# Part of one basis combination moved into earlier pauses, the segment-maximum's key work moved ahead of the weight preparations, and the last biases added as rounded matmul rows

## The chip, the cores and the metric

One Trainium2 chip, one of its cores. Five engines run their own instruction streams and meet at semaphores: PE (matmul and transposes), DVE (VectorE), ACT (ScalarE), POOL (GpSimd) and SP, which here only issues DMAs. The metric is the device time of one execution in microseconds (us), as the median of several runs. Positions in the trace are us from the first instruction.

## The reference

Four graph layers in a row on 625 nodes with 512 features and 10,000 edges sorted by destination; each adds its result to `x`. What the change touches are the first and the last:

```python
# L0: attention over edges, softmax per destination node, then a feed-forward part
logits = einsum('ehd,ehd->eh', q[src], k[dst]); a = logits + dist_attn + path_attn
mx = segment_max(a, dst)                       # the "maximum"
e = exp(a - mx[dst]); s = segment_sum(e, dst); msg = v[src] * (e / s[dst])
...
# L3: two relational layers; w[r] is a sum over 30 bases of 512 x 512
w = einsum('rb,bio->rio', att, basis)          # r = 2 relations
...
return agg + x @ root + bias
```

The second layer of L3 uses `basis2`, `att2` and `bias2`. Nothing in `w` depends on the nodes, so the kernel forms it whenever an engine is free. L2's weights are also prepared ahead (products and transposes of `W_self`, `W_fwd`, `W_bwd`).

## The kernel before

Nodes are five tiles of 128 (`NC`), edges 84 tiles of 128 (`NT`), feature columns four blocks of 128 (`K4`). All order is written by hand: each engine's stream is a straight list, and semaphores name what it waits for.

The stretch of the change is the first third. In order of the program:

- **Sorting and projections.** DVE ranks edges in batches (`inner_ranks`, `places`); PE computes q and k in two blocks `project(0)` and `project(1)` of 64 matmuls each, between which DVE takes the next ranks. POOL sends each batch's 16 columns of edge rows to DRAM with indirect DMAs (L727, 80 in all), then loads the sorted table `att` (L733).
- **Pairs.** All node pairs' products go to DRAM by SP (`pair_d`, ten DMAs of 1.25 MB, L593).
- **v.** Five tiles; DVE adds the bias (L1314) and SP stores `v_d` (L599). PE has two PSUM slots for them, so tile m+2 waits until DVE took tile m. SP first issues the first three of the L2 weight loads (`early_in`, L597).
- **Gathers.** POOL gathers 84 tiles of logits from `pair_d` (L740), then v rows (L749), 21 tiles ahead of their use.
- **Run of bases.** `combine_run` (L1328) multiplies the 30 lower halves of `basis2` by two factors each into `acc_run`: two instructions of 1,024 columns for each base (L1335 for the first, L1341 for the others). SP loads them into three buffers, 0.5 MB each (`load_run`, L583). SP issues base 0 to 2 after `v_d`; bases 3 to 29 stand behind a wait for the landing of `v_d` and of the pairs, and behind the load of `Wo` (L606).
- **Preparations.** At the same time PE works on the 15 parts in `EARLY`: eight are 16 transposes (L1822), six are 16 f32 products (L1820), and the last product is cut in three (L1804). ACT takes each result out of PSUM (`take_early`, L869) and issues the weight load for the part three later (L871). A product needs the transposed part before it.
- **Maximum.** Logits and segment keys are turned to 112 rows by twelve transposes (L1921); ACT copies both out (L909, L911). DVE makes penalties where the key changes (L1363 to L1365), runs two scans (L1369, L1370), collects the ends of each row, and PE turns these (L1928). DVE then joins the rows on one lane (L1383 to L1404), PE turns the carries back (L1933), and DVE scans again, takes the maximum and subtracts it.
- **Messages.** PE adds 84 weighted tiles (L1976) of v rows.

In the last two layers (l = 3, 4 of `LAYERS`) `own` starts the sums of layer 3 with an f32 matmul of one row of ones and the bias (L2185); `bias2` is instead added to `xs` by one POOL instruction (L804) in layer 4's preparation.

## Time and profile before

| | us |
|---|---|
| median of 3 runs | 1359.07 |
| lowest, highest | 1354.73, 1360.41 |
| the profiled execution | 1360.03 |
| its span, first to last instruction | 1358.3 |
| TensorE clock granted over it (share of full) | 0.93 |

| engine | busy, us | share |
|---|---|---|
| PE | 1174.0 | 86% |
| DVE | 862.2 | 63% |
| ACT | 436.0 | 32% |
| POOL | 424.6 | 31% |

The shares average over stages with different limits, so the argument reads single stretches: who was idle, and which row ended that. A timeline row is start, duration, engine, line, operation, and in brackets the idle time before it with what ended it. A chain row is start, duration and what the end of the program hung on at that time.

### The profile page before, as it was taken

What the parts mean: (1) busy time and instruction counts of PE and PEld (TensorE: products, weight loads), DVE (VectorE), ACT (ScalarE), POOL (GpSimd) and SP (SyncE); (2) the same over time, 40 slices, a digit from 0 to 9 for tenths busy, and PEclk for the clock granted to TensorE, in tenths of its full rate; (3) what the DMA queues carried; (4) which work ended last, traced back from release to release, by engine and by line L of the source; (5) the groups of instructions that cost most, each with busy time, mean ns of one, the idle gap of its engine ahead of it and who ended that gap; (6) DMA issues with size and microseconds to landing.
All of it is one profiled execution on the core that took longest, in us unless ns stands there. A gap on an engine that the chain in (4) does not pass through costs nothing.

```text
span 1358.3 us, 15202 instructions
## 1 busy us (share of the span) xinstructions
PE 1174.0 (86%) x5421; PEld 822.1 (61%) x5440; DVE 862.2 (63%) x1405; ACT 436.0 (32%) x618; POOL 424.6 (31%) x405
## 2 busy tenths in 40 slices
PE   5597768847997799999897998899799998989996
PEld 4364344423543477544457997568587886778884
DVE  7618425767775649786569996636869697482211
ACT  2315121212111722100328995543232324233320
POOL 3878677772774001110037771000000000010000
PEclk8799888977999899999978999999799999899898
DMA  6215799994764024531124112034545554222001
GB/s 213 54 12 193 232 383 344 332 341 172 244 180 123 31 78 128 193 99 63 49 48 147 43 44 97 1 112 165 184 147 208 176 195 172 102 84 102 0 0 38
DMA packets 74337, 187.82 MB, mean 138 GB/s; under 512 B 14423, under 2 KB 17468, under 8 KB 69029
## 3 DMA queue, kind: packets, MB, share of 16 engines
q1 hardware_dynamic: 45044, 100.34, 21.3%
q0 software_dynamic: 21600, 64.66, 15.8%
q10 hardware_dynamic: 7632, 22.02, 4.4%
q8 instruction: 38, 0.62, 0.2%
q14 instruction: 23, 0.18, 0.0%
HBM read 149.93 MB, written 36.97 MB: 138 GB/s over the span
## 4 chain that ended last, share of the span: by engine, by line
PE 57%; DVE 17%; DMA 11%; ACT 5%; issue 5%; POOL 2%; SPq 2%; ACTq 0%; DVEq 0%; PEldq 0%
PE ps L2160 25%; DMA work<-in_L_gnn_basis 7%; PE ps L2065 5%; PE ps L2123 4%; PE ps L2055 4%; PE ps L1976 3%; DVE aux L1676 3%; PE ps L1878 3%; DVE work L1341 2%; POOL aux L749 2%; PE ps L2035 2%; DMA pair_d<-aux 2%; PE ps L1851 2%; DMA xs<-in_x 2%; PE ps L2108 2%
## 5 line engine op out<-in xcount | busy, mean ns | idle before, releaser
L2160 PE MATMUL ps<-work_r,hT_r 128*128 128x512 f32 x600 | 195.9, 408 | 2.1 <-DVE att_r L1648 1.4
L2160 PEld LDWEIGHTS ps<-work_r,hT_r 128*128 128x128 f32 x600 | 114.9, 194 | 32.9 <-issue 4.7
L2160 PE MATMUL ps<-work_r,att_r 128*128 128x512 f32 x300 | 121.2, 404 | 0.0
L727 POOL DMA_INDIRECT etab_d<-aux,edge x80 | 99.2, 1241 | 49.2 <-issue 49.2
L1652 DVE TENSOR_TENSOR bT_r<-bT,fT_r 128x512 fp32r<-128x512 f32 x50 | 38.7, 774 | 106.7 <-ACT fT_r L1065 106.7
L1676 DVE SCALAR_TENSOR_TENSOR aux<-aux,attb 128x1024 f32<-128x1024 f32 x84 | 103.1, 1278 | 2.4 <-DMA aux<-in_L_gnn_basis 2.4
L1341 DVE SCALAR_TENSOR_TENSOR work<-work,attb 128x1024 f32<-128x1024 f32 x58 | 72.0, 1296 | 42.1 <-DMA work<-in_L_gnn_basis 42.1
L2160 PE MATMUL ps<-fT_r,wA_r 128*128 128x512 f32 x250 | 87.0, 416 | 10.8 <-DVE bT_r L1652 10.8
L740 POOL DMA_INDIRECT lg<-pair_d,reli x84 | 86.2, 1026 | 29.1 <-issue 25.3
L1976 PE MATMUL ps<-work,hT_r 128*128 128x512 f32 x168 | 85.5, 642 | 8.8 <-DVE work L1424 6.5
L1820 PE MATMUL ps<-wA 128*128 128x512 f32 x160 | 77.3, 646 | 16.0 <-DMA wA<-in_L_gnn_W_bwd 6.2
L1494 DVE TENSOR_SCALAR work<-iota,srcf,flag 128x640 bf16<-128x640 f16 x168 | 64.3, 447 | 37.8 <-PE ps L2036 37.6
L2160 PE MATMUL ps<-fT_r,aux_r 128*128 128x512 f32 x250 | 80.7, 400 | 3.6 <-DVE bT_r L1652 3.6
L2123 PE MATMUL ps<-work_r 128*128 128x256 f32 x280 | 70.3, 288 | 10.3 <-DVE wA_r L1582 10.3
L749 POOL DMA_INDIRECT aux<-v_d,srcx x64 | 70.4, 1100 | 19.5 <-issue 18.6
L2065 PE MATMUL ps<-wA,aux 128*128 128x512 f32 x160 | 73.1, 599 | 1.3 <-issue 1.3
L2123 PE MATMUL ps<-wA_r,work_r 128*128 128x256 f32 x280 | 69.3, 288 | 0.0
L782 POOL DMA_DIRECT2D work<-early_d x9 | 5.4, 602 | 200.3 <-PE ps L2160 134.4
L1820 PEld LDWEIGHTS ps<-wA 128*128 128x128 f32 x160 | 32.6, 207 | 57.7 <-issue 46.3
L2160 PEld LDWEIGHTS ps<-work_r,att_r 128*128 128x128 f32 x300 | 58.1, 194 | 14.4
L2160 PEld LDWEIGHTS ps<-fT_r,wA_r 128*128 128x128 f32 x250 | 49.4, 197 | 26.1 <-DVE bT_r L1652 12.7
L778 POOL DMA_INDIRECT fT<-u_d,dstx x36 | 40.6, 1127 | 77.4 <-DMA u_d<-bT 66.7
(396 smaller groups left out, 2646.0 us busy)
## 6 DMA issues: line engine op xcount, KB each, us to landing
aux<-in_L_gnn_basis SPq DMA_DIRECT2D x44, 512.0 KB, 3.9
work<-in_L_gnn_basis SPq DMA_DIRECT2D x30, 512.0 KB, 9.5
fT<-in_L_gnn_basis POOLq DMA_DIRECT2D x24, 512.0 KB, 4.4
wA<-in_L_gnn_basis SPq DMA_DIRECT2D x22, 512.0 KB, 3.9
work<-early_d POOLq DMA_DIRECT2D x9, 1024.0 KB, 5.9
wA<-in_L_gnn_W_self ACTq DMA_DIRECT2D x7, 1024.0 KB, 14.9
pair_d<-aux SPq DMA_DIRECT2D x5, 1280.0 KB, 14.0
early_d<-work ACTq DMA_DIRECT2D x5, 1024.0 KB, 16.9
```

The costliest lines, as they stand in the source:

```text
L727: pool.indirect_dma_start(out=etab_d, out_offset=bass.IndirectOffsetOnAxis(ap=row[:, t:t + 1], axis=0), in_=etab[:, t, :], in_offset=None) ...
L740: pool.indirect_dma_start(out=lg[:, t, :], out_offset=None, in_=pair_d, in_offset=bass.IndirectOffsetOnAxis(ap=reli[:, t:t + 1], axis=0)). ...
L749: pool.indirect_dma_start(out=ring[t % RING], out_offset=None, in_=v_d, in_offset=bass.IndirectOffsetOnAxis(ap=srcx[:, t:t + 1], axis=0)). ...
L1341: ins = dve.scalar_tensor_tensor(acc_run[:, r], bas_run[b % 3], factor, acc_run[:, r], ALU.mult, ALU.add)
L1494: last = dve.tensor_scalar(hotS[:, 4 * k + j, :], iota16[:, :], srcf[:, at], flag[:, r, at], ALU.is_equal, ALU.mult)
L1676: ins = dve.scalar_tensor_tensor(acc[:, r], bas[u], factor, acc[:, r], ALU.mult, ALU.add)
L1820: last = pe.matmul(to[:, k], w[:, o, k * P:(k + 1) * P], early_s[:, o, :], start=o == 0, stop=o == K4 - 1)
L1976: pe.matmul(ps[:, bass.ds(c * 512, D)], one, msg[:, j, :], start=False, stop=False, skip_group_check=True)\
L2055: last = pe.matmul(o, w, h[:, k, nodes], start=k == i == 0, stop=(k, i) == (K4 - 1, 2))
L2065: last = pe.matmul(plan.slot(ps, "ffn2", m), node(g1T, j, m), w2s[:, j, :], start=j == 0, stop=j == 15)
L2123: last = pe.matmul(ps[:, 512 * m:512 * m + NF], hotL[k][:, j, m * P:(m + 1) * P], part[:, 4 * k + j, :], start=False, stop=False)
L2160: last = pe.matmul(o, lhsT, rhs, start=start and n == 0, stop=stop and n == 2)
```

## The change

It has five parts.

1. **Bases.** The first 12 bases (`AHEAD_RUN`) load into buffers that are free from the start, behind the last parameter loads on SP. DVE combines 0 to 5 after `places(1)` and 6 to 11 after `places(2)`. The loads of 12 to 16 stand behind the pair stores, ahead of the first weight loads; DVE combines 12 to 15 between the tiles of v, base 16 after the keys are laid out, base 17 inside the key work, 18 to 29 behind it.
2. **Keys first.** Keys are turned, copied, made into penalties and seams before the preparations; the logits come after all of them. `s_ends`, `s_soft`, `s_akT` and `s_endT` count one or two events more.
3. **Last part whole.** `ASKING` is 15: the last product is prepared as the others, not cut in three.
4. **Bias rows.** `rows_r` holds each bias of L3 as a rounded row and its rest, multiplied by two rows of ones in rounded f32, in layer 3 and in layer 4.
5. **Buffers** of the ends, chains and carries move.

```diff
+AHEAD_RUN = 12
@@ SP
+            load_run(range(AHEAD_RUN))
             for n in range(2 * NC):
...
+            sp.wait_ge(s_place, 5)
+            load_run(range(AHEAD_RUN, AHEAD_RUN + 5))
             sp.wait_ge(s_pre_job, pre.number("v", NC - 1))
             for n in range(3):
                 sp.dma_start(early_in[n], early_source(n)).then_inc(s_early_in[n], 16)
             sp.wait_ge(s_pre_dve, NC)
             sp.dma_start(v_d.rearrange("(m p) n -> p m n", p=P), vf).then_inc(s_v_out, 16)
-            sp.wait_ge(s_place, 5)
-            load_run(range(3))
             sp.wait_ge(s_v_out, 16)
...
-            load_run(range(3, NBASE))
+            load_run(range(AHEAD_RUN + 5, NBASE))
@@ POOL, layer 4
-                if l == LAYERS - 1:
-                    pool.wait_ge(s_norm, seen(5))
-                    pool.wait_ge(s_l3par, 6 * 16)
-                    pool.tensor_tensor(xs[:, :, :], xs[:, :, :], rows[:, 1, :].unsqueeze(1).to_broadcast([P, NC, D]), ALU.add).then_inc(s_added, 1)
@@ ACT
+            act.wait_ge(s_akT, 1)
+            act.activation(kT, ps[0:112, 2048:2048 + 768], ACT.Copy).then_inc(s_ak, 1)
             for part in range(ASKING):
                 take_early(part)
@@ DVE
             places(1)
+            dve.wait_ge(s_attb, 32)
+            combine_run(range(6))
             inner_ranks(range(8, 12))
             places(2)
+            combine_run(range(6, AHEAD_RUN))
...
                 dve.tensor_tensor(vf[:, m, :], pre.slot(ps, "v", m)[:, 0:D], bv, ALU.add).then_inc(s_pre_dve, 1)
+                if m < NC - 1:
+                    combine_run([AHEAD_RUN + m])
...
             dve.tensor_copy(kp.rearrange("p g t h -> p t g h"),
                             segk[:, :].rearrange("p (t g) -> p t g", g=TG).unsqueeze(3).to_broadcast([P, TT, TG, H])).then_inc(s_soft, 1)
+            first = AHEAD_RUN + NC - 1
+            combine_run(range(first, first + 1))
+            dve.wait_ge(s_ak, 1)
             step(dve.memset(pen[:, :], 0.0))
...
+            combine_run(range(first + 1, first + 2))
             dve.wait_ge(s_endT, 1)
+            dve.tensor_copy(*turned_ends(2, 3)).then_inc(s_ends, 1)
...
+            combine_run(range(first + 2, NBASE))
@@ DVE, layer 0
+                    step(dve.tensor_copy(ones_r, ones[0:2, :]))
+                    for j in range(2):
+                        step(dve.tensor_copy(bias_upper, rows[0:2, j, :]))
+                        step(dve.tensor_tensor(rows_r[0:2, j, :], rows[0:2, j, :], bias_upper, ALU.subtract))
+                        step(dve.tensor_copy(rows_r[0:1, j, :], bias_upper[0:1]))
@@ PE
-            prepare(range(ASKING))
+            pe.wait_ge(s_soft, 1)
+            for g in range(TG):
+                last = pe.transpose(ps[0:112, 2048 + g * P:2048 + (g + 1) * P], kp[:, g].rearrange("p t h -> p (t h)"), ident[:, :])
+            last.then_inc(s_akT, 1)
+            prepare(range(1))
+            pe.wait_ge(s_ends, 1)
+            turn_ends((2, 3, 4))
+            pe.wait_ge(s_ak, 1)
+            pe.wait_ge(s_ends, 2)
+            prepare(range(1, ASKING))
@@ PE, own
-                if l == 3:
-                    pe.wait_ge(s_l3par, 6 * 16)
-                    pe.matmul(o, ones[0:1, :], rows[0:1, 0, :], start=True, stop=False)
+                if l >= 3:
+                    pe.matmul(o, ones_r, rows_r[0:2, l - 3, :], start=True, stop=False)
```

Three places show the new order. On SP's queue, before, from the last pair store:

```order
L593 DMA pair_d<-aux 128x2560 [waits s_pair_dve,s_pair_act]
L597 DMA wA<-in_L_gnn_W_self 128x4x512 [waits s_pre_job]
L597 DMA wA<-in_L_gnn_W_self 128x4x512
L597 DMA wA<-in_L_gnn_W_fwd 128x4x512
L599 DMA v_d<-aux 128x5x512 [waits s_pre_dve]
L583 DMA work<-in_L_gnn_basis 128x2x512 [waits s_place]
L583 DMA work<-in_L_gnn_basis 128x2x512 x2
L606 DMA aux<-in_L_gnn_Wo 128x4x512 [waits s_pair_out2,s_pair_out3,s_pair_out1,s_wo,s_pair_out0,s_v_out]
L583 DMA work<-in_L_gnn_basis 128x2x512 [waits s_bas_used0]
```

The same place of the changed kernel; the last row loads base 17:

```order
L597 DMA pair_d<-aux 128x2560 [waits s_pair_dve,s_pair_act]
L586 DMA work<-in_L_gnn_basis 128x2x512 [waits s_place]
L586 DMA work<-in_L_gnn_basis 128x2x512 x2
L586 DMA work<-in_L_gnn_basis 128x2x512 [waits s_bas_used0]
L586 DMA work<-in_L_gnn_basis 128x2x512 [waits s_bas_used1]
L603 DMA wA<-in_L_gnn_W_self 128x4x512 [waits s_pre_job]
L603 DMA wA<-in_L_gnn_W_self 128x4x512
L603 DMA wA<-in_L_gnn_W_fwd 128x4x512
L605 DMA v_d<-aux 128x5x512 [waits s_pre_dve]
L610 DMA aux<-in_L_gnn_Wo 128x4x512 [waits s_pair_out2,s_pair_out3,s_pair_out1,s_wo,s_pair_out0,s_v_out]
L586 DMA work<-in_L_gnn_basis 128x2x512 [waits s_bas_used2]
```

Bases 12 to 16 now stand ahead of the weight loads, and base 17 stands behind the wait for `v_d` and the load of `Wo`, where base 3 stood.

On DVE, before, from the segment keys (`segk`) on:

```order
L1326 SCALAR_TENSOR_TENSOR segk<-dstx,att 128x84 [waits s_dve]
L1335 TENSOR_SCALAR work<-work,attb 128x1024 [waits s_bas_in0,s_attb,s_dve]
L1335 TENSOR_SCALAR work<-work,attb 128x1024
L1341 SCALAR_TENSOR_TENSOR work<-work,attb 128x1024 [waits s_base_done,s_bas_in1]
L1341 SCALAR_TENSOR_TENSOR work<-work,attb 128x1024 [waits s_bas_used0]
```

And in the changed kernel, behind the copy of the keys (L1287 is a base's instruction, the copy on L1378 takes the turned ends of the keys):

```order
L1287 SCALAR_TENSOR_TENSOR work<-work,attb 128x1024 [waits s_base_done,s_bas_in1]
L1287 SCALAR_TENSOR_TENSOR work<-work,attb 128x1024 [waits s_bas_used0]
L1369 MEMSET work 112x769 [waits s_ak]
L1370 TENSOR_TENSOR work<-work 112x767 [waits s_dve]
L1371 TENSOR_SCALAR work<-work 112x767 [waits s_dve]
L1372 COPY ends<-work 112x1 [waits s_dve]
L1373 COPY ends<-work 112x1
L1374 TENSOR_REDUCE ends<-work 112x1
L1375 MEMSET work 1x224
L1287 SCALAR_TENSOR_TENSOR work<-work,attb 128x1024 [waits s_base_done,s_bas_in2,s_dve]
L1287 SCALAR_TENSOR_TENSOR work<-work,attb 128x1024 [waits s_bas_used1]
L1378 COPY edge<-ps 1x336 [waits s_endT]
```

The key work, formerly behind all thirty bases, has bases 16 and 17 inside it.

On PE, before, behind the last tile of v:

```order
L1822 MATMUL ps<-ident,wA 128x128 [waits s_early_in0,s_pre_dve]
L1822 MATMUL ps<-ident,wA 128x128 x15
L1822 MATMUL ps<-ident,wA 128x128 [waits s_early_in1]
L1822 MATMUL ps<-ident,wA 128x128 x15
L1820 MATMUL ps<-wA 128x512 [waits s_early_taken,s_early_in2]
```

And in the changed kernel:

```order
L1920 MATMUL ps<-ident,work 112x128 [waits s_soft,s_pre_dve]
L1920 MATMUL ps<-ident,work 112x128 x5
L1831 MATMUL ps<-ident,wA 128x128 [waits s_early_in0]
L1831 MATMUL ps<-ident,wA 128x128 x15
L1925 MATMUL ps<-ident,ends 1x112 [waits s_ends]
L1925 MATMUL ps<-ident,ends 1x112 x2
L1831 MATMUL ps<-ident,wA 128x128 [waits s_early_in1,s_ends,s_ak]
L1831 MATMUL ps<-ident,wA 128x128 x15
L1829 MATMUL ps<-wA 128x512 [waits s_early_taken,s_early_in2]
```

Between the first and the second preparation PE now waits for DVE (`s_ends`, twice).

## Rows read from the trace of the kernel before

**Rows 1.** Chain of waits, in order of time: start, us, what.
```profile
175.14 16.86 DMA work<-in_L_gnn_basis
...
302.28 2.62 DVE work L1341 x2
```
**Rows 2.** Timeline of DVE, four places of the first third.
```profile
81.08 0.35 DVE L1175 SCALAR_TENSOR_TENSOR ps<-ps,edge,earlier 125x125 f32<-125x125 f32 x1 [15.49 <-PE ps L1775]
...
103.66 0.36 DVE L1175 SCALAR_TENSOR_TENSOR ps<-ps,edge,earlier 125x125 f32<-125x125 f32 x1 [15.46 <-PE ps L1775]
...
153.22 0.69 DVE L1314 TENSOR_TENSOR aux<-ps,wA 128x512 f32<-128x512 f32 x1 [1.07 <-PE ps L1905]
...
258.20 14.92 DVE L1341 SCALAR_TENSOR_TENSOR work<-work,attb 128x1024 f32<-128x1024 f32 x12 [3.46 <-DMA work<-in_L_gnn_basis]
```
**Rows 3.** Timeline of SP's DMA issues.
```profile
146.37 0.32 SPq L593 DMA_DIRECT2D pair_d<-aux  x1
166.88 0.94 SPq L597 DMA_DIRECT2D wA<-in_L_gnn_W_self  x2
...
185.88 0.37 SPq L606 DMA_DIRECT2D aux<-in_L_gnn_Wo  x1
```
**Rows 4.** DMA issues: count, KB each, median us.
```profile
aux<-in_L_gnn_basis SPq DMA_DIRECT2D x44, 512.0 KB, 3.9
...
pair_d<-aux SPq DMA_DIRECT2D x5, 1280.0 KB, 14.0
...
v_d<-aux SPq DMA_DIRECT2D x1, 1280.0 KB, 17.4
```
**Rows 5.** Timeline of PE, the preparations and the maximum's first transposes.
```profile
181.52 14.00 PE L1820 MATMUL ps<-wA 128*128 128x512 f32 x32 [0.24 <-DMA wA<-in_L_gnn_W_fwd]
...
205.70 16.27 PE L1820 MATMUL ps<-wA 128*128 128x512 f32 x32 [6.18 <-DMA wA<-in_L_gnn_W_bwd]
...
230.32 15.70 PE L1820 MATMUL ps<-wA 128*128 128x512 f32 x32 [4.29 <-DMA wA<-in_L_gnn_W_fwd]
...
250.39 15.67 PE L1820 MATMUL ps<-wA 128*128 128x512 f32 x32 [2.63 <-ACT wA L869]
...
306.90 2.81 PE L1921 MATMUL ps<-ident,work 128*112 128x128 f32 x12 [18.98 <-DVE work L1359]
```
**Rows 6.** Timeline of ACT, the take of part 13.
```profile
288.57 1.88 ACT L869 ACTIVATE wA<-ps 128x2048 f32<-128x2048 f32 x1 [0.42 <-ACT hT L869]
```
**Rows 7.** Timeline of DVE, maximum up to the first message.
```profile
313.10 1.76 DVE L1369 TENSOR_TENSOR_SCAN bT<-work 112x768 f32<-112x768 f32 x1
...
321.05 0.73 DVE L1383 COPY work<-ps 1x560 f32<-1x560 f32 x1 [3.09 <-PE ps L1928]
...
335.14 1.90 DVE L1424 TENSOR_TENSOR work<-fT,lg 128x512 f32<-128x512 f32 x3 [0.26 <-PEq L1966]
```
**Rows 8.** Page, costliest groups: POOL's scatters; busy us, mean ns, idle before.
```profile
L727 POOL DMA_INDIRECT etab_d<-aux,edge x80 | 99.2, 1241 | 49.2 <-issue 49.2
```
**Rows 9.** Timeline of POOL: one scatter, two gathers of logits.
```profile
146.66 3.81 POOL L727 DMA_INDIRECT etab_d<-aux,edge  x1 [0.30 <-issue]
...
258.48 1.82 POOL L740 DMA_INDIRECT lg<-pair_d,reli  x1 [0.30 <-issue]
...
281.91 1.41 POOL L740 DMA_INDIRECT lg<-pair_d,reli  x1 [0.30 <-issue]
```
**Rows 10.** Chain of waits in layer 3: start, us, what.
```profile
1148.57 3.49 PE ps L2160 x15
...
1165.78 1.05 PE ps L2185 x2
```
**Rows 11.** Timelines of POOL, DVE and PE in layer 3 to 4.
```profile
1201.11 5.66 POOL L804 TENSOR_TENSOR xs<-xs,rows 128x2560 f32<-128x2560 f32 x1 [26.15 <-PE ps L2160]
...
1202.36 4.96 DVE L1652 TENSOR_TENSOR bT_r<-bT,fT_r 128x512 fp32r<-128x512 f32 x1 [1.75 <-ACT fT_r L1065]
...
1207.37 0.79 PE L2160 MATMUL ps<-fT_r,aux_r 128*128 128x512 f32 x1 [3.56 <-DVE bT_r L1652]
```

More of the change, by code:

```diff
@@ L307, in build @@
         parows = fT[0:40, 0:P]
-        rows = sb("rows", [P, 2, D])
+        rows, rows_r = sb_twice("rows", [P, 2, D])
         bv = wA[:, 6144:6144 + D]
@@ L1274, in factors, with combine_run @@
                 dve.scalar_tensor_tensor(nmr[:, m:m + 1], mv[:, m, 0:1], -1.0, rstd[:, m:m + 1], ALU.mult, ALU.mult).then_inc(s_stat, 1)
+            def combine_run(bases):
+                for b in bases:
+                    dve.wait_ge(s_bas_in[b % 3], 16 * (b // 3 + 1))
+                    for r in range(2):
+                        factor = attb[:, 1, b + r * NBASE:b + r * NBASE + 1]
+                        if b == 0:
+                            ins = dve.tensor_scalar(acc_run[:, r], bas_run[b], factor, None, ALU.mult)
+                        else:
+                            if r == 0:
+                                dve.wait_ge(s_base_done, b)
+                            else:
+                                dve.wait_ge(s_bas_used[(b - 1) % 3], (b - 1) // 3 + 1)
+                            ins = dve.scalar_tensor_tensor(acc_run[:, r], bas_run[b], factor, acc_run[:, r], ALU.mult, ALU.add)
+                        ins.then_inc((s_base_done, s_bas_used[b % 3])[r], 1)
             sort_begin()
@@ L1796, in sort_look @@
                 last.then_inc(s_looked, 1)
-            def prepare_last(columns):
-                kind, l = EARLY[-1]
-                w, to = early_in[EARLY_IN[-1]], early_banks(len(EARLY) - 1)
-                for k in columns:
-                    for o in range(K4):
-                        last = pe.matmul(to[:, k], w[:, o, k * P:(k + 1) * P], early_s[:, o, :], start=o == 0, stop=o == K4 - 1)
-                return last
             def prepare(parts):
```

126 lines of the change are left out of this document (56 added, 70 removed).

## The prediction, made before the changed kernel ran

> **What bounds the kernel now.** I read the chain of waits first, then the timelines of the engines it names. From 175 to 305 the chain alternates between the landing of a base and its two instructions on DVE [rows 1]; PE, which has done 14 of its 15 preparations by then, stands idle for 18.98 us until DVE has laid out the logits [rows 5]. Then follows the maximum, and the first message starts at 335.14 [rows 7]. The last gather of logits is issued at 281.91 [rows 9], so without the bases DVE could begin at about 285, and 22 us look free. But the preparations are a second chain close behind: part 13 is taken out at 288.57 + 1.88 = 290.45 [rows 6], and part 14, now made whole, costs 15.67 us on PE [rows 5] and 1.88 us on ACT before the logits may be turned: 290.45 + 0.2 + 17.6 = 308.2. That is later than the 306.90 of before. So the gain of the moved bases is nearly spent by the new order of part 14, and the question is when PE's chain of preparations starts and how fast it runs.
>
> **Twelve bases in the pauses.** A base costs DVE 14.92 / 6 = 2.49 us [rows 2]. Six are 14.9 us; the two pauses are 15.49 and 15.46 us [rows 2]. With three buffers a reload has two bases' time, 5.0 us, and lands in 3.9 us where nothing else loads [rows 4]. They fit with half a microsecond to spare each. If they don't, DVE's ranks are late one for one, and the pairs behind them. Between nothing and 2 us I take **+0.5 us**.
>
> **Bases 12 to 15 between the tiles of v.** SP issues 12 behind the last pair store at 146.37, which lands by about 160 (14.0 us at the median, rows 4) [rows 3, 4]. The first v tile is added at 153.22 [rows 2], so DVE now waits there some 7 us for base 12; then come four times a base and a tile (2.49 + 0.69): the last tile at about 174 instead of 168. PE's last v tile waits for DVE's third, so the first weight loads go out at about 170 instead of 166.88.
>
> **PE now waits for base 17.** This is the new wait. PE's second preparation needs the ends of the keys off PSUM, DVE's copy of these stands behind base 17, and SP issues base 17 only after `v_d` has landed and behind `Wo`. Before, the weight loads went out at 166.88 and `v_d` had landed by 185.88 [rows 3]: 3 + 1.25 MB in 19.0 us, 0.224 MB a us, with the wait in `v_d`'s row of 17.4 us [rows 4]. Now: 170 + 17 to 19, about 188 (two ACT loads fewer compete, since PE has only made part 0). `Wo` and base 17, 1.5 MB, take 3.9 us at the least and 6.7 at that rate: 193 to 195. Two instructions, the copy and the signal add 3.3. PE's second preparation starts at **T = 199**; behind PE stand parts 1 to 14, and the logits behind them. Bounds: 190 (`v_d` in 11 us, base in 4) and 208 (below).
>
> **From T to the first message.** Before, from the start of part 2 at 181.52 [rows 5] to part 13 taken at 290.45 [rows 6] it was 108.9 us. Part 1 adds about 3.5 (12 transposes took 2.81 after an idle time, rows 5), part 14 and its take 17.8. Two products waited for their weights, 6.18 and 4.29 us, where the later ones wait only 2.63 for ACT [rows 5]; with fewer base loads beside them up to 5.2 us go, and I take 4. So all is taken at T + 126.2. Then six transposes (half of 2.81), ACT's copy and signals: scans at T + 128.9. Before, the first scan was 22.0 us ahead of the first message (313.10 to 335.14, rows 7). Two scans end at 316.6, and DVE had the ends at 321.05: of these 4.4 us about 0.8 remain, since penalties, key ends and the slice of part 14 are out of the way. Five small seam instructions, three fifths of the copy, and ACT's last take in front of its exponential save about 2.4 more. 22.0 - 6.0 = 16.0. First message at T + 144.9 = 344 instead of 335.1: **+8.9 us**, and the 84 messages behind it shift as a block. The other bases end long before: 12 x 2.49 = 30 us after T.
>
> **Bias rows.** In layer 3 the f32 bias costs 1.05 us a tile [rows 10]. A rounded matmul costs 3.49 / 15 = 0.23 [rows 10]; no row shows one of two rows, so its bounds are 0.23 and 1.05, and I take 0.23, as the columns are the same. Tile 0's saving is lost, for PE then waits for ACT's normalised tile; four times 0.82 is 3.3. Layer 4 has five new ones, 1.2. Net **-2.1 us** (bounds -2.1 and +5.3). Seven small DVE instructions in layer 0 prepare them; six of them have half of a base instruction's columns, 0.6 us each, 3.7 in sum, while PE works through a side's product. Taken as 0, at most 3 if the cover fails.
>
> **The POOL addition goes.** It holds POOL from 1201.11 for 5.66 us, and a DVE subtraction that takes 0.69 elsewhere takes 4.96 beside it; PE waits 3.56 us for that [rows 11], and after the pause it runs at the lower clock for some instructions, which I price at 1.2. With the subtraction done at 1203.1 PE doesn't stop: **-4.8 us** (bounds -3.5 and -5).
>
> **Sum.** +8.9 + 0.5 - 2.1 - 4.8 = +2.5. The profiled execution took 1360.03, 1.0 above the median; the difference is applied to the median: 1359.07 + 2.5, about **1362 us**.
>
> **The rivals.**
> *Short hold, faster.* `v_d` and base 17 move at close to the rate of an idle queue: T = 190. For it: DVE frees POOL and ACT issues two transfers of 1 MB less. Against: the 0.224 MB a us, and the store of `v_d` is issued later than before. First message at 335, so 0 + 0.5 - 6.9: 1352.6.
> *No hold, faster.* The change would do what it says: keys done at about 182, T = 185, first message at 330: -5.2 + 0.5 - 6.9 gives 1347.5. It needs base 17 before `v_d` has landed, which the order excludes.
> *Late table, slower.* DVE's base instructions block POOL's scatters. One scatter takes 1.241 us in the mean [rows 8], but 3.81 while DVE adds the bias rows to the nodes [rows 9]; one gather of logits takes 1.82 as DVE starts a row of bases at 258.20, another 1.41 [rows 2, 9]. If each scatter must wait for a gap between two base instructions, its pace goes from about 1.5 to 2.49 us: 12 scatters in the 30 us of the two pauses lose 1 us each, four more in v's stage. Table, keys and penalties are then 12 to 16 us late. By this path T would be the end of the table's work, about 178 where the base chain starts in rows 1, plus 12 us (the keys' transposes, copy and penalties, two bases, the copy of the ends): 190, so 9 us are to spare against base 17, and beyond that it sets T: 178 + 16 + 12, about 206, and 208 at most. At 208: +17.9 + 0.5 - 6.9, 1370.6.
>
> The Trainium skill (SBUF — State Buffer, section Who interferes with whom) says that a DVE instruction with two SBUF inputs contends with a GpSimd instruction that reads SBUF, but infers that descriptor generation isn't held by it. By that rule the late table costs nothing and the sum stays +2.5; by the 3.81 us row it may reach +11.5. The trace disagrees with the inference, and I leave the rival a real chance.
>
> **Chances and range.** Forecast 0.52, short hold 0.20, no hold 0.05, late table 0.20, other 0.03. From the low of the short hold to the late table: 1351 to 1371. A measurement can tell about 0.5%, 6.8 us: below 1352.3 lie no hold, half of the short hold and a tail, 0.19; above 1365.9 the late table and a tail of the forecast, 0.26; the rest is 0.55.
>
> **What would show it.** PE idle from about 185 to 199 ahead of part 1, released by DVE's copy of the turned ends, and this by base 17's landing; the logits' transposes at about 325, not waiting for DVE; first message near 344; no DVE instruction near 5 us in layer 3. If PE's idle is released by the keys' own instructions instead, the late table is right. The forecast is wrong if T lies under 194 or over 204, or if the preparations take a different time than 126 us from there.

## The result and the profile after

| | before | changed |
|---|---|---|
| median of 5 runs | 1358.95 us | 1372.2 us |
| lowest to highest | 1350.6 to 1360.41 | 1369.44 to 1378.5 |
| profiled execution | 1360.03 | 1378.5 |

The ratio is 1.0125, 95% interval 1.0091 to 1.0159: **slower by 17 us** (12 to 22); the two medians stand 13.3 us apart, inside that. The prediction was 1362 us, no measurable change, with a range up to 1371. It was wrong. The profiled execution is the longest of the five. From the last norm of the trace (1178.07 us in it, 1156.66 before) to the first subtraction into `att_r` (1263.50, 1249.80 before) it is 7.7 us faster than before, and it loses 4.8 of them again behind that, where the granted clock is 0.90 between 1298 and 1328 us and 0.98 at the same place of before. Four later kernels with the same bias rows (e12, e13, e15, w4) take 3.2 us less for the first of these stretches and 3.3 less for the second. So the end of this trace overstates the loss by some 6 us, which is what it lies above the median.

The loss is made in the first quarter. Timeline of VectorE (DVE) of the changed kernel: start, us, line, operation, idle time before it and what ended it. `places(k)` ends a step of the sort in which DVE ranks edges. The two groups of bases:

```profile
57.13 1.41 DVE L1281 TENSOR_SCALAR work<-work,attb 128x1024 f32<-128x1024 f32 x2
58.46 12.04 DVE L1287 SCALAR_TENSOR_TENSOR work<-work,attb 128x1024 f32<-128x1024 f32 x10
...
78.90 14.43 DVE L1287 SCALAR_TENSOR_TENSOR work<-work,attb 128x1024 f32<-128x1024 f32 x12
...
117.12 0.35 DVE L1173 SCALAR_TENSOR_TENSOR ps<-ps,edge,earlier 125x125 f32<-125x125 f32 x1 [15.52 <-PE ps L1793]
```

In before the two long pauses ended at 81.08 and 103.66 [rows 2]: they began at 65.6 and 88.2, behind `places(2)` and `places(3)`. The first group runs from 57.13 to 70.5, behind `places(1)`, and there DVE of before waits only 1.67 us:

```profile
58.51 0.36 DVE L1175 SCALAR_TENSOR_TENSOR ps<-ps,edge,earlier 125x125 f32<-125x125 f32 x1 [1.67 <-PE ps L1775]
```

The second group does lie in a pause, the first of the two. The other pause, now 15.52 us, is still there, at the end of the sort, but nothing lies in it. So the next two steps of the ranks, TensorE's counts that go with them and the dense pair products come late. The same kernel further on, SyncE's issues (SPq), then DVE from the v tiles to the copy of the turned ends:

```profile
160.31 0.32 SPq L597 DMA_DIRECT2D pair_d<-aux  x1
160.69 20.84 SPq L586 DMA_DIRECT2D work<-in_L_gnn_basis  x5
188.82 0.92 SPq L603 DMA_DIRECT2D wA<-in_L_gnn_W_self  x2
...
204.89 43.93 SPq L586 DMA_DIRECT2D work<-in_L_gnn_basis  x13
```
```profile
166.00 0.68 DVE L1331 TENSOR_TENSOR aux<-ps,wA 128x512 f32<-128x512 f32 x1
175.66 2.48 DVE L1287 SCALAR_TENSOR_TENSOR work<-work,attb 128x1024 f32<-128x1024 f32 x2 [8.97 <-DMA work<-in_L_gnn_basis]
...
211.78 2.48 DVE L1287 SCALAR_TENSOR_TENSOR work<-work,attb 128x1024 f32<-128x1024 f32 x2 [11.45 <-issue]
214.18 0.49 DVE L1378 COPY edge<-ps 1x336 f32<-1x336 f32 x1
```

The last pair store leaves at 160.31 instead of 146.37 [rows 3]; DVE waits 8.97 us for base 12 between the first two v tiles; and base 17, issued at 204.89 behind `Wo`, holds the copy of the turned ends until 214.18. TensorE (PE) in the same kernel, the first pair product, its second preparation, the last one, the logits' turn and the first product of the message stage:

```profile
124.57 16.51 PE L1906 MATMUL ps<-fT,aux 64*128 64x320 f32 x96 [3.96 <-issue]
...
214.76 3.65 PE L1831 MATMUL ps<-ident,wA 128*128 128x128 f32 x16 [14.16 <-issue]
...
317.48 15.67 PE L1829 MATMUL ps<-wA 128*128 128x512 f32 x32 [2.63 <-ACT wA L869]
335.27 0.84 PE L1944 MATMUL ps<-ident,work 128*112 128x128 f32 x6 [2.12 <-ACT work L869]
...
354.77 1.98 PE L1972 MATMUL ps<-work 128*128 128x512 bf16 x5 [4.82 <-issue]
```

PE stands 14.16 us ahead of its second preparation. The logits' turn no longer waits for DVE, as [rows 5] did with 18.98 us, but for ScalarE's (ACT's) take of the last preparation: the bound has moved from DVE's run of bases to the chain of preparations, and that ends later. The message stage (here and below: the start of PE's first message product) starts at 354.77; in the trace of before the product that answers to it starts at 336.40 us. The prediction counted to the first message instruction on DVE, which stands 1.2 us ahead of it in both (353.54 and 335.14).

### The profile page after: what moved, and what is told of

Read it like the earlier page. It is cut to its first block, busy times and chain, and to the rows that moved or that the text cites. A ratio compares the mean times of both kernels' runs of the same rounds, so it can differ in the third digit from the quotient of the medians.

```text
span 1376.8 us, 15205 instructions
## 1 busy us (share of the span) xinstructions
PE 1176.4 (85%) x5421; PEld 827.3 (60%) x5440; DVE 859.7 (62%) x1413; ACT 436.3 (32%) x618; POOL 422.6 (31%) x404
## 4 chain that ended last, share of the span: by engine, by line
PE 59%; DVE 17%; DMA 7%; issue 6%; ACT 6%; POOL 2%; SPq 1%; ACTq 0%; DVEq 0%; PEldq 0%
PE ps L2176 22%; PE ps L1829 6%; PE ps L2081 5%; PE ps L2139 4%; PE ps L2071 4%; DVE aux L1689 3%; PE ps L1992 3%; PE ps L1887 3%; POOL aux L753 2%; PE ps L2051 2%; PE ps L1860 2%; DMA pair_d<-aux 2%; PE ps L2124 2%; DMA xs<-in_x 1%; DMA work<-in_L_gnn_basis 1%
## 5 line engine op out<-in xcount | busy, mean ns | idle before, releaser
L731 POOL DMA_INDIRECT etab_d<-aux,edge x80 | 104.3, 1304 | 50.0 <-issue 49.1
L1829 PE MATMUL ps<-wA 128*128 128x512 f32 x192 | 89.1, 624 | 12.5 <-ACT wA L869 7.9
L1665 DVE TENSOR_TENSOR bT_r<-bT,fT_r 128x512 fp32r<-128x512 f32 x50 | 34.2, 689 | 101.7 <-ACT fT_r L1063 101.6
L1287 DVE SCALAR_TENSOR_TENSOR work<-work,attb 128x1024 f32<-128x1024 f32 x58 | 71.0, 1286 | 34.4 <-DMA work<-in_L_gnn_basis 22.9
L2139 PE MATMUL ps<-work_r 128*128 128x256 f32 x280 | 70.5, 288 | 10.5 <-DVE wA_r L1595 10.5
L1829 PEld LDWEIGHTS ps<-wA 128*128 128x128 f32 x192 | 38.0, 201 | 60.0 <-issue 54.9
```

The costliest lines, as they stand in the source:

```text
L731: pool.indirect_dma_start(out=etab_d, out_offset=bass.IndirectOffsetOnAxis(ap=row[:, t:t + 1], axis=0), in_=etab[:, t, :], in_offset=None) ...
L1287: ins = dve.scalar_tensor_tensor(acc_run[:, r], bas_run[b], factor, acc_run[:, r], ALU.mult, ALU.add)
L1829: last = pe.matmul(to[:, k], w[:, o, k * P:(k + 1) * P], early_s[:, o, :], start=o == 0, stop=o == K4 - 1)
L2139: last = pe.matmul(ps[:, 512 * m:512 * m + NF], hotL[k][:, j, m * P:(m + 1) * P], part[:, 4 * k + j, :], start=False, stop=False)
```

## The experiments

The runs were made in sets, each on one chip and with the kernel before beside the others. Three sets ran like the first comparison (before 1355 to 1356 us): w0 and w4; e11 to e13; e14 and e15. In the other sets the median of before was 1482 to 1497 us and those of the others 1474 to 1519; they are called disturbed here, their ratios are compared among themselves alone, and their traces are read up to the second preparation. These landmarks are from the undisturbed traces, one for each kernel (us; PE starts):

| kernel | first pair product | second preparation | logits' turn | message stage | ratio to before |
|---|---|---|---|---|---|
| before | 111.22 | | 306.90 | 336.40 | 1 |
| w0, before, wide reads | 111.14 | | 300.41 | 329.66 | 0.9972 (0.9939 to 1.0004) |
| e14, before, bias rows | 111.18 | 176.91 | 302.22 | 330.47 | 0.9965 (0.9945 to 0.9985) |
| changed | 124.57 | 214.76 | 335.27 | 354.77 | 1.0125 (1.0091 to 1.0159) |
| e12, groups later | 110.74 | 202.73 | 322.11 | 341.73 | 1.0038 (1.0010 to 1.0066) |
| e13, base 17 behind | 125.80 | 200.82 | 323.45 | 343.18 | 1.0028 (1.0003 to 1.0053) |
| w4, both, wide reads | 110.94 | 190.77 | 313.17 | 332.70 | 0.9983 (0.9950 to 1.0016) |
| e11, last one inside | 111.69 | 191.33 | 296.93 | 322.66 | 0.9883 (0.9849 to 0.9916) |
| e15, third delay | 111.98 | | 300.46 | 322.59 | 0.9898 (0.9869 to 0.9926) |

**The groups one step later (e1, e7, e12).** The theory: the group of bases behind `places(1)` lies in no pause. The rival: DVE's base instructions slow POOL's scatters, wherever they lie.

```
             places(1)
-            dve.wait_ge(s_attb, 32)
-            combine_run(range(6))
             inner_ranks(range(8, 12))
             places(2)
-            combine_run(range(6, AHEAD_RUN))
+            dve.wait_ge(s_attb, 32)
+            combine_run(range(6))
             inner_ranks(range(12, 16))
             places(3)
+            combine_run(range(6, AHEAD_RUN))
```

> The changed kernel with its two groups of bases each moved one step of the sort later on VectorE: bases 0 to 5 behind places(2) instead of places(1), bases 6 to 11 behind places(3). In the trace of before the pauses of 15.49 and 15.46 us stand there, behind places(2) and places(3), and behind places(1) only 1.67 us. My theory: the 13.4 us by which the changed kernel's dense pair products start late (111.22 to 124.57 us) come from a group of 14.4 us in a place without a pause. Then they start at 111 to 113 us again and the kernel takes 1372.2 - 13 = 1359 us (1356 to 1363); PE's second preparation, at 214.76 us in the changed kernel, starts at 201 to 203 us. Rival, contention: POOL's scatters take 2.08 us beside the base instructions instead of 1.19 us, and that is the loss. They still lie beside the groups here, so the pair products would still start 6 us or more late and the kernel would take 1366 us or more.

> The kernel of e1 (groups of bases one step later on VectorE), in undisturbed conditions: the kernel before takes 1355 us here, as in the first comparison. In e1's trace the pair products start at 111.4 us and PE's second preparation at 203.5, against 124.6 and 214.8 in the changed kernel. Theory: 11 to 13 us come off the time, 0.8 to 1.0% less than the changed kernel's ratio of 1.0125, so 1.002 to 1.006. Rival, from w0 and w4 (the kernel with both moves isn't faster than before where I had said 12 us): something behind the preparations' start takes back what is gained there; then 1.008 or more.

> e1's kernel (groups one step later alone) again, for a call that may be undisturbed. Theory as for e7: ratio 1.002 to 1.006. Rival: 1.008 or more.

e1's ratio was 1.0156 (1.0092 to 1.0219) and e7's 1.0077 (1.0036 to 1.0117), both disturbed: e1 missed what was expected of its time, and e7 lies between theory and rival. Their traces have the landmarks of the theory all the same, pair products at 111.37 and 111.26 and second preparations at 203.53 and 203.78. e12 took 1360.71 us against 1356.06, 1.0038. DVE and PE of e12, the groups and what follows:

```profile
67.10 12.04 DVE L1287 SCALAR_TENSOR_TENSOR work<-work,attb 128x1024 f32<-128x1024 f32 x10
...
88.25 14.44 DVE L1287 SCALAR_TENSOR_TENSOR work<-work,attb 128x1024 f32<-128x1024 f32 x12
```
```profile
110.74 15.59 PE L1906 MATMUL ps<-fT,aux 64*128 64x320 f32 x96 [3.69 <-issue]
...
202.73 3.65 PE L1831 MATMUL ps<-ident,wA 128*128 128x128 f32 x16 [12.58 <-issue]
...
341.73 2.36 PE L1972 MATMUL ps<-work 128*128 128x512 bf16 x6 [4.47 <-issue]
```

The pair products start 13.8 us sooner than in the changed kernel, as in before, the second preparation 12.0 and the message stage 13.0 sooner; the time falls by 0.87% of 1356, 12 us. That is a difference of two ratios from two sets; with their intervals joined it is 12 us give or take 6. Shown: the place of the groups costs 13 us at the message stage, and the time agrees. The rival falls, since the scatters beside the groups took 2.09 us here too and the pair products were on time.

**Base 17 behind the copy (e2, e8, e13).**

```
-            combine_run(range(first + 1, first + 2))
             dve.wait_ge(s_endT, 1)
             dve.tensor_copy(*turned_ends(2, 3)).then_inc(s_ends, 1)
...
-            combine_run(range(first + 2, NBASE))
+            combine_run(range(first + 1, NBASE))
```

> The changed kernel with base 17's combination moved on VectorE from ahead of the copy of the turned ends (for which TensorE's second preparation waits) to behind the seam's steps. In the changed kernel the copy stands at 214.18 us, behind base 17 at 211.78 us, which waited 11.45 us for its load; TensorE waited 14.16 us for it. My theory: the copy runs at 201 to 202 us, TensorE's second preparation starts at 202 to 203 us instead of 214.76, and 12 us come off the first message product: 1372.2 - 12 = 1360 us (1357 to 1364). Rival, the run goes on binding: the preparations' own inputs queue behind the bases, or the logits' landing (308 to 309.4 us in the changed kernel) ends last; then the gain is 5 us or less, 1367 us or more.

> The kernel of e2 (base 17 behind the copy of the turned ends), undisturbed. In e2's trace the copy stands at 200.4 us instead of 214.2. Theory: 8 to 12 us less than the changed kernel, ratio 1.003 to 1.007. Rival: the second preparation starts earlier, but its inputs and the stores come at the pace of the DMA queues, so the last preparation ends when it did: 1.010 or more, with longer waits of TensorE between the preparations.

> e2's kernel (base 17 behind the copy of the turned ends alone) again. Theory as for e8: ratio 1.003 to 1.007. Rival: 1.010 or more.

e2: 1.0178 (1.0108 to 1.0249), e8: 1.0101 (1.0064 to 1.0138), both disturbed and both where the rival had put the time, though their second preparations start at 200.99 and 201.06. e13: 1359.91 us, 1.0028. Its copy and PE's second preparation:

```profile
200.22 0.50 DVE L1377 COPY edge<-ps 1x336 f32<-1x336 f32 x1 [0.38 <-PE ps L1924]
```
```profile
200.82 3.50 PE L1830 MATMUL ps<-ident,wA 128*128 128x128 f32 x16 [0.70 <-issue]
```

The hold of 14.16 us is 0.70, the second preparation starts 13.9 us sooner, the message stage 11.6, and the time falls by 0.97%, 13 us give or take 6. In the changed kernel the rows put PE's 14.16 us and DVE's 11.45 us down to "issue", so that base 17 is what both awaited is shown by this run and not by those rows. The hold was real and is a second cost of the same size.

**Both (e3, e3 again, e9) and wide reads (w0, w4).** e3 has both edits. w0 and w4 are before and e3 with `"b (c p k) n -> b c p k n"` for relation 2's bases and `"(p k) n -> p k n"` for the preparations' sources; values stand in another order, bytes don't change.

> Both moves together: the groups behind places(2) and places(3), and base 17 behind the seam's steps. My theory: two independent delays, so the gains add: 1372.2 - 13 - 12 = 1347 us (1342 to 1352), 12 us below the kernel before; TensorE's second preparation starts at 188 to 191 us, the message products at 331 to 334 us. Rival, the next thing is late: with the preparations done by 310 us the logits' gathers on POOL and DVE's run end last, and the message products start at 340 us or later; then 1354 us or more.

> The same kernel as e3_both, once more: both moves, the two groups of bases behind places(2) and places(3), and base 17 behind the seam's steps. In e1, e2 and e3 the stretch to 195 us went as in the theory (pair products at 111 us, second preparation at 194 us), but from there every kernel of that call, the kernel before too, was 130 us longer than in the first comparison, and TensorE's single products stood 2.8 us apart. Theory: without that disturbance the two gains add, 0.991 of the time before (1347 us against 1359). Rival, the logits end last: 0.997 or more.

> The kernel of e3 (both moves), undisturbed; w4_both_wide, which differs in how weights and bases are read alone, took 0.998 of the time before. Theory of added gains: 0.991. Rival, given back between the second preparation and the last: 0.997 to 1.002, with TensorE waiting 10 us or more in all for inputs that land late beside the bases' loads and the logits' gathers.

> The kernel before, but the halves of relation 2's bases, and the forward and backward weights of the preparations, are read with the rows that one partition gets standing together: 4 KB and 8 KB in a piece instead of 2 KB. The bytes and the instructions are the same, the values are in another order, so that part of the output isn't the reference's. Meant as a base for pairs outside the disturbed stretch: in e1 to e6 every kernel, the one before too, lost 130 us between 195 us and 340 us, where 141 packets of 2 KB start per us in the first comparison. Theory: the number of packets per us sets that loss; with some half of them it shrinks, and the kernel takes 60 us or more less than the kernel before on the same chip (1495 us), or, where the disturbance is absent, the same as it within 5 us. Rival: the loss has another source, then the two take the same on this chip within 15 us.

> The same reading in pieces of 4 and 8 KB on the kernel with both moves (e3_both); the values are in another order again. Theory, where the disturbance shrinks: 12 us (8 to 16) less than w0_before_wide, since the groups of bases lie in the real pauses, base 17 holds nothing, and 6.9 us of the bias rows come on top of an unchanged or shorter end of the softmax. Rival: the message products don't start earlier than in w0_before_wide, since the logits or the preparations' inputs end last; then 5 us less or none.

Disturbed: 1.0133 (1.0056 to 1.0210), 1.0072 (1.0024 to 1.0120) and 0.9993 (0.9954 to 1.0031); the same kernel in three sets, and the spread of 1.4% shows how little one such ratio says. w4 took 1352.48 us against before's 1354.94, and w0 1352.93. That set was an undisturbed one, so whether fewer packets mend the disturbance was not answered. In w4:

```profile
190.77 3.64 PE L1830 MATMUL ps<-ident,wA 128*128 128x128 f32 x16 [0.70 <-issue]
...
297.08 13.97 PE L1828 MATMUL ps<-wA 128*128 128x512 f32 x32 [2.61 <-ACT wA L869]
313.17 0.84 PE L1943 MATMUL ps<-ident,work 128*112 128x128 f32 x6 [2.12 <-ACT work L869]
...
332.70 1.98 PE L1971 MATMUL ps<-work 128*128 128x512 bf16 x5 [4.85 <-issue]
```
```profile
290.60 0.86 DVE L1390 SCALAR_TENSOR_TENSOR lg<-lg,att 128x672 f32<-128x672 f32 x1 [45.71 <-DMA lg<-pair_d,reli]
```

The delays add: 22.1 us come off the message stage of the changed kernel (13.0 and 11.6 alone), and 1.42%, 19 us, off the time. w4 has the wide reads too, but they aren't what did it: e11 below has both edits without them, and its second preparation starts at 191.33, w4's at 190.77. My forecast that w4 would take 12 us less than w0 fell, though; it took 0.5 less. The ratio that e9's rival named came true, but not its reason: PE waits only 3.63 and 2.15 us for weights in w4. Against w0, which has the same reads, w4's message stage starts 3.0 us later. The rows say why: DVE has the logits ready at 292, while PE still makes the last preparation until 311, and only then turns them. In before that product lay inside the softmax's waits.

**The last preparation back inside (e11).** From e3. PE turns the logits into the odd banks behind the last but one preparation; the last one's 16 steps run in four pieces; ACT takes it behind the copy of the logits.

```
+            prepare(range(1, ASKING - 1))
...
+            pe.wait_ge(s_early_taken, ASKING - 1)
             for g in range(TG): ...
+            prepare_last(range(0, 5))
             pe.wait_ge(s_ends, 3)
             turn_ends((0, 1))
+            prepare_last(range(5, 7))
...
+            prepare_last(range(7, 12))
...
+            prepare_last(range(12, 16)).then_inc(s_early_job, 1)
```

> The kernel with both moves (e3), and the last preparation put back into the softmax as in the kernel before: TensorE turns the logits behind the last but one preparation (into the odd banks), ScalarE copies them, and the last product's 16 steps run in pieces of 5, 2, 5 and 4 between the softmax's turns. In w4's trace (undisturbed) the last but one preparation is taken at 294.7 us, the logits had been ready at 292.0, and the first message product starts at 334; the last preparation, 297.1 to 313, stood between. Theory: the product is hidden in the softmax's waits (16.5 us of them), so the message products start at 314 to 318 us, 17 us sooner than w4's and 20 sooner than in the kernel before; ratio to before 0.982 to 0.987. Rival, from the finding that both moves won less than their delays: POOL's gathers of v (288.5 us on, 84 of 1.25 us) then end last, the message loop runs at their pace, and the ratio is 0.992 or more.

1341.17 us against 1356.06: **0.9883**, the fastest kernel of this study, 16 us faster than before (11 to 20), where 18 to 24 were expected. PE and ACT of e11:

```profile
296.93 1.28 PE L1952 MATMUL ps<-ident,work 128*112 128x128 f32 x6 [2.67 <-ACT wA L869]
298.00 5.75 PE L1940 MATMUL ps<-wA 128*128 128x512 f32 x10
...
311.86 3.61 PE L1940 MATMUL ps<-wA 128*128 128x512 f32 x8
322.66 2.36 PE L1985 MATMUL ps<-work 128*128 128x512 bf16 x6 [7.18 <-issue]
```
```profile
315.57 1.88 ACT L869 ACTIVATE work<-ps 128x2048 f32<-128x2048 f32 x1 [16.51 <-PE ps L1940]
...
317.86 1.28 ACT L913 ACT_TABLE_LOAD   x1 [0.41 <-ACT work L869]
```

The logits are turned 16.2 us sooner than in w4, the message stage starts 10.0 sooner. The rest of it went to an order of mine: on ACT the take stands ahead of the exponential's table load, so the exponentials begin at 319.26 although DVE had their input at 312.9.

**The third delay (e15).** From e11: bases 12 to 14 behind the v tiles and the others behind the seam's steps, two preparations ahead of the keys' turn, ACT's take behind the exponentials.

```
-                if m < NC - 1:
-                    combine_run([AHEAD_RUN + m])
+            combine_run(range(AHEAD_RUN, AHEAD_RUN + 3))
...
+            prepare(range(2))
+            pe.wait_ge(s_early_taken, 2)
             pe.wait_ge(s_soft, 1)
...
+            act.activation(parts[:, :, 0, :], lga[:, :, :], ACT.Exp).then_inc(s_prob, 1)
+            take_early(ASKING - 1)
```

> e11 with what its trace still shows. (1) VectorE waits 9.5 us for base 12 ahead of the second v tile, so TensorE's v products pause 7.8 us and the weights' loads are issued at 176.0 us instead of 166.9: bases 12 to 14 come behind the v tiles, and the others behind the seam's steps. (2) TensorE's first two preparations wait for the keys' turn at 184.1 us: they go ahead of it, the seam's turns stand on either side of the third. (3) ScalarE takes the last preparation (315.6 us) ahead of the exponentials, which TensorE's marks then await for 7.2 us: it takes it behind them. Theory: the message products start at 314 to 318 us instead of 325, and the ratio falls from 0.988 to 0.982 (0.979 to 0.985). Rival: the logits, ready at 292.6 us, and POOL's gathers end last whatever comes ahead of them; then only (3) counts, 5 us, and the ratio is 0.985 or more.

1341.39 us, 0.9898: the same as e11. The time is where the rival put it, though the 5 us that it granted aren't there either. The rows of POOL and DVE show what was lost. First e11, then e15:

```profile
174.05 1.71 POOL L737 DMA_DIRECT2D att<-etab_d  x3 [1.99 <-DMA etab_d<-aux,edge]
179.41 1.02 POOL L744 DMA_INDIRECT lg<-pair_d,reli  x1 [3.66 <-DVE reli L1341]
```
```profile
179.33 1.70 POOL L737 DMA_DIRECT2D att<-etab_d  x3 [5.90 <-DMA etab_d<-aux,edge]
186.92 1.02 POOL L744 DMA_INDIRECT lg<-pair_d,reli  x1 [5.89 <-DVE reli L1342]
```
```profile
185.62 0.18 DVE L1340 CAST srcx<-att 128x28 int32<-128x28 f32 x1 [10.85 <-DMA att<-etab_d]
...
299.01 0.86 DVE L1391 SCALAR_TENSOR_TENSOR lg<-lg,att 128x672 f32<-128x672 f32 x1 [31.90 <-DMA lg<-pair_d,reli]
```

The v tiles were through at 167.6 us and the weights' loads left at 166.90 instead of 176.01. But they, and the store of `v_d` behind them, are then in flight with the last scatters, whose landing POOL awaits 5.90 us instead of 1.99, and with the table's load. The first gather of logits goes out 7.5 us later, and DVE has the logits at 299.9 instead of 292.0. So PE turns the logits 3.5 us later (300.46 against 296.93), and from there to the message stage it is 22.1 us instead of 25.7, since the exponentials, no longer behind the take, begin at 317.05 instead of 319.26. The two effects cancel: 322.59 against 322.66. That the loads are the cause was not tested apart. In the changed kernel POOL awaits the same landing for 6.26 us, with the weights' loads not yet issued but the last pair store (160.31) and bases 12 to 16 on their way; so if it is traffic that delays it, the weights aren't the only one that does.

**The bias rows alone (e4, e10, e14).** Before, with rounded rows, layer 3's product on them, layer 4's product in place of POOL's addition:

```
+                    dve.wait_ge(s_l3par, 6 * 16)
+                    step(dve.tensor_copy(ones_r, ones[0:2, :]))
...
-                    pool.tensor_tensor(xs[:, :, :], xs[:, :, :], rows[:, 1, :].unsqueeze(1).to_broadcast([P, NC, D]), ALU.add).then_inc(s_added, 1)
...
-                if l == 3:
-                    pe.wait_ge(s_l3par, 6 * 16)
-                    pe.matmul(o, ones[0:1, :], rows[0:1, 0, :], start=True, stop=False)
+                if l >= 3:
+                    pe.matmul(o, ones_r, rows_r[0:2, l - 3, :], start=True, stop=False)
```

> The kernel before with only the part on the bias rows: both rounded in layer 0, layer 3's product on the split rows, layer 4's bias added by a product in the own() pass too, and POOL's addition of 5.66 us with the VectorE instruction of 4.96 us beside it gone. My theory, as predicted: 2.1 us less in layer 3 and 4.8 us less at layer 4's start, 1359 - 6.9 = 1352 us (1349 to 1355). Rival: the idle times at those places are taken up again behind them, since the chain of layer 4 ends on other work; in the traces the stretch from layer 3's last norm to the end is 201.6 us before and 198.7 us after, so 1359 - 3 = 1356 us (1354 to 1358).

> The kernel of e4 (before with the bias rows' part alone), undisturbed. As predicted 6.9 us less, 0.995. Rival, by the traces' stretch from layer 3's last norm to the end (201.6 us before, 198.7 after) 2.9 us in layer 4 and up to 2.1 in layer 3: 0.9963 to 0.998.

> The kernel of e4 (before with the bias rows' part alone), for a call that may be undisturbed. Predicted: 6.9 us less, 0.995. Rival: in w4, e11, e12 and e13 the time stands 2 to 5 us lower against before than the start of the message products does, so the part brings 3 us: 0.997 to 0.999.

0.9942 (0.9903 to 0.9981) and 0.9939 (0.9905 to 0.9973) disturbed, 0.9965 (0.9945 to 0.9985) undisturbed: 4.8 us less, between 2 and 7.5. Theory and rival both reach into that interval, so it doesn't decide between them. In the trace of the changed kernel the instruction of 4.96 us [rows 11] is gone from its line, page, costliest groups:

```profile
L1665 DVE TENSOR_TENSOR bT_r<-bT,fT_r 128x512 fp32r<-128x512 f32 x50 | 34.2, 689 | 101.7 <-ACT fT_r L1063 101.6
```

**One input (e5) and the changed kernel again (e6).** e5 is e3 with `dve.tensor_scalar(acc_run[:, r], bas_run[b], factor, None, ALU.mult)` for bases 1 to 11; it leaves out the sum over them.

> As e3_both, but bases 1 to 11 are combined by a multiplication of the base alone (one input of 128x1024 from SBUF instead of two); the sum over those bases is left out, so that relation's weight isn't the reference's. In all kernels POOL's scatters take 2.08 us beside the groups of base instructions and 1.19 us elsewhere. Theory: what slows them is VectorE reading two inputs, so here they take 1.19 us all through (mean of the 80 scatters 1.24 us, as before, instead of 1.30), and one base instruction takes 0.8 us instead of 1.2. Rival: any long VectorE instruction on SBUF slows them; then they stay at 1.4 us or more beside the groups.

> The changed kernel, unchanged, in the same conditions as e1 to e4, in which every kernel, the one before too, takes 130 us more between 195 us and 340 us than in the first comparison. Theory: the delays of 13.4 us (groups of bases) and 12 us (base 17 ahead of the copy) are real in these conditions too: the ratio to before is 1.0125 or more, and e1's 1.0156, e2's 1.0178 and e3's 1.007 to 1.013 lie below it. Rival: the disturbed stretch swallows what comes ahead of it, and all four have the same ratio.

POOL's scatters beside the first group, e12 (two inputs), then e5 (one):

```profile
69.74 2.09 POOL L731 DMA_INDIRECT etab_d<-aux,edge  x1 [0.30 <-issue]
72.13 2.09 POOL L731 DMA_INDIRECT etab_d<-aux,edge  x1 [0.30 <-issue]
```
```profile
69.46 1.24 POOL L731 DMA_INDIRECT etab_d<-aux,edge  x1 [0.30 <-issue]
71.00 1.24 POOL L731 DMA_INDIRECT etab_d<-aux,edge  x1 [0.30 <-issue]
```

The rival falls: these one-input instructions of 128x1024 leave the scatters at 1.24 us inside a group (single ones at its edges took 1.44 and 1.61), where the two-input ones make them 2.09. The edit changes more than the number of inputs, though: the instruction is another one, and takes 0.79 us instead of 1.20. e6 gave 1.0131 (1.0051 to 1.0212), disturbed. The theory was that e1, e2 and e3 lie below it; e1 and e2 lie above, and all the intervals overlap, so in those conditions the times could not tell the delays apart. The trace could: e6's pair products start at 124.53 and its second preparation at 215.00, as in the changed kernel's first trace.

## Why the prediction was wrong

**"Twelve bases in the pauses", +0.5 us: the step that failed.** The durations were right: 14.43 us for six bases against 14.9 forecast. The place was not. [rows 2] gave the pauses by their ends, 81.08 and 103.66, and I took them for those behind `places(1)` and `places(2)`; they are behind `places(2)` and `places(3)`. No row between `places(1)` and the next rank instruction was read. The prediction's "They fit with half a microsecond to spare each" holds for the second group alone; the first lies where the wait is 1.67 us. The pair products came 13.35 us late, and e12 shows 13 us of it at the message stage and 12 (give or take 6) in the time. The text even named the price ("DVE's ranks are late one for one, and the pairs behind them"), but as a matter of the loads' speed.

**"PE now waits for base 17", T = 199: right within 4 us.** T is the start of PE's second preparation. With the groups in the pauses it is 202.73 (e12), in the changed kernel 214.76 = 202.7 + 12, beyond the 204 that the prediction named as its sign of being wrong. The hold was counted in the forecast (8.9 us in all for the front), and e13 puts its price at 11.6 us on the message stage and 13 us of time. That PE's idle hangs on DVE's copy and this on base 17 was forecast and is what e13 shows. That T came so close is in part luck. DVE waited 8.97 us for base 12 where I had said 7, but PE then stood 6.06 us between the v tiles, which I had not counted: the weights' loads left at 188.82, 175.5 without the 13.35, and not at 170. From there to T it was 25.9 us instead of the 29 forecast, and the two errors cancel in part.

**From T to the first message: 144.9 forecast, 138.8 measured** (214.76 to 353.54). The preparations took less, 120.4 us to the last take instead of 126.2: the products waited 2.89 and 1.74 us for weights where before had 6.18 and 4.29 [rows 5] and the forecast kept 6.5, and two products ran 14.0 us instead of 15.67. From the scans to the message it was 16.55 us, with 16.0 forecast. So without the first error the message would have come at 341 where I said 344.

**The base of the sum, 335.14.** I took the first message of before from one execution. Two other traces with the same front (w0, e14) have the message stage at 329.66 and 330.47, 6.3 us sooner than the 336.40 of the profiled execution, mostly because DVE's run of bases ends sooner (the logits' turn starts at 300.41 and 302.22 instead of 306.90). Against that, the front costs 6.3 us more than the difference I formed. This is the second error, of size and not of mechanism. It rests on two traces, and w0 has the wide reads. But the times support it: measured from e14, which has the bias rows like the changed kernels, the message stages of e12 and of the changed kernel stand 11.3 and 24.3 us later, and their ratios 0.73% and 1.60% higher, 10 and 22 us. From 336.40 they would stand only 5.3 and 18.4 us later.

**Bias rows and POOL's addition, -6.9:** -4.8 measured, with -6.9 inside its interval. One term is mis-sized by the rows: I took 0.23 us for a product of two rows, and in the trace the next product starts 0.43 us behind it, as here in the changed kernel:

```profile
1182.45 0.50 PE L2200 MATMUL ps<-rows_r,wA_r 2*128 2x512 f32 x1
1182.88 0.74 PE L2176 MATMUL ps<-work_r,hT_r 128*128 128x512 f32 x2
```

By the prediction's own count that makes 4 x 0.62 saved and 5 x 0.43 added, -0.3 instead of -2.1, and with the -4.8 that it forecast for the addition an estimate of -5.1.

**The sum again** (an estimate, each term from one or two traces)**:** 2.5, and 12.85 for the groups (13.35 less the 0.5), 6.3 for the base, -3.8 for the rest of the front, 2.1 for the bias rows: +19.9, against the measured 17 (12 to 22). With the groups in their pauses it is +7.1, against 5.2 (1.4 to 8.9) for e12.

**Late table: not it.** This rival had DVE's instructions slow POOL's scatters and the sorted table come late. The scatters did slow to 2.08 us, a pace of 2.39, close to the 2.49 that the rival had; but POOL had idle time to give, the table's instructions were done at 193.4, and PE's wait ended with base 17 (e13). The Trainium skill (SBUF — State Buffer, section Who interferes with whom) infers that descriptor generation isn't held by the second input's port. Here 1.19 us became 2.09 beside instructions with two inputs and 1.24 beside those with one, so the measurement stands against the inference, as far as these indirect DMAs go. The rival had the right contention and the wrong weight.

Short hold and no hold fell with T. What the prediction said of the last preparation in its first paragraph was right (308.2 against 306.90, the gain "nearly spent"), and e11 shows that it is what keeps the change from paying once its delays are gone: w4 stands at 0.9983, e11 at 0.9883.

## What to carry to other kernels

Before work is put into a pause, find the instruction that the program's order puts directly ahead of it, and read the idle time in front of the very instruction that will follow the inserted ones; a pause named by its end is easily placed one step off. When a chain of waits is broken, look for the second chain behind it (here the preparations, then the logits' gathers): in this kernel the last preparation lay inside the old wait, and with it put ahead of what waited the logits' turn came 16 us later (w4 against e11). And a sum whose two ends come from one execution carries that execution's lateness; e14's trace, with the same front, stands 6 us sooner.

## What the runs showed of the hardware

- POOL's scatters (indirect DMA issues of 125 rows) take 2.09 us beside DVE's `scalar_tensor_tensor` of 128x1024 with two SBUF inputs, 1.24 beside `tensor_scalar` with one, 1.19 alone (e12, e5). With the 0.30 us between them the pace goes from 1.49 to 2.39 us. Here it costs nothing, since POOL waits later: 4.08 us ahead of the last two scatters in e12.
- With 3 MB of weights and the store of `v_d` issued 9 us sooner, the wait for the scatters' landing was 3.9 us longer and the first gather 7.5 us later (e15 against e11). That the one caused the other was not tested apart.
- TensorE's first 35 us behind the trace's last norm had a granted clock of 0.80 in the changed kernel's trace, 0.85 in e14 and e11, and 0.90 in e12, e13, e15 and w4, all with the same instructions there. From that norm to the first subtraction into `att_r` it took 85.4, 83.8 and 82.2 to 82.3 us: one execution's clock moved the end by up to 3 us in this stretch alone.
- In the disturbed sets PE's single products had 1.8 us and more of idle time between them from some point behind 195 us on (210 in e3), without a releaser in the trace, while DVE and POOL kept their durations. The disturbed sets ran on chips 3, 6 and 1, the undisturbed ones on 7, 13 and 5, and no chip was in both; what causes it stays open. Two such rows of e3:

```profile
218.43 1.01 PE L1828 MATMUL ps<-wA 128*128 128x512 f32 x1 [1.79 <-issue]
221.23 1.01 PE L1828 MATMUL ps<-wA 128*128 128x512 f32 x1 [1.79 <-issue]
```
